# Scores on all eight 64x32 tiles of TensorE, and the feed-forward's sums in the free halves of the attention outputs' banks

## What is computed

```
def attn_layer(x, Wqkv, qs, ksc, Wo):            # 16 heads of 64
    q, k, v = heads(x @ Wqkv)
    q = l2norm(q) * qs;  k = l2norm(k) * ksc
    q, k = rotary(q), rotary(k)
    out = local_attention(q, k, v)               # windows of 32 queries, each sees 64 keys
    return out.reshape(b, n, INNER) @ Wo
def ffn_layer(x, g, bln, W1, b1, W2, b2):
    mu = x.mean(-1, keepdims=True)
    var = ((x - mu) ** 2).mean(-1, keepdims=True)
    xn = (x - mu) / jnp.sqrt(var + 1e-05) * g + bln
    a, gate = jnp.split(xn @ W1 + b1, 2, -1)
    return a * jax.nn.gelu(gate, approximate=False) @ W2 + b2
for i in range(DEPTH):                           # 6 layers, run twice in all
    x = attn_layer(shift_tokens(x), ...) + x
    x = ffn_layer(shift_tokens(x), ...) + x
```

## Time and profile before

| | us |
|---|---|
| median of 3 runs (lowest, highest) | 3282.68 (3281.99, 3286.73) |
| the profiled execution's own time | 3285.78 |
| its span, first to last instruction | 3284.0 |
| PE busy, share of the span | 3149.2 (96%) |
| DVE, POOL, ACT busy | 2675.4 (81%), 2593.5 (79%), 2355.0 (72%) |

### The profile page before, as it was taken

How to read it: one execution, slowest core, us unless ns; L and a number is a source line. 1 busy time by engine, 2 the same in 40 slices (tenths; PEclk the granted TensorE clock), 3 DMA queues, 4 the chain that set the end, 5 groups by cost and what they waited for, 6 DMA issues and landing times.

```text
span 3284.0 us, 149930 instructions
## 1 busy us (share of the span) xinstructions
PE 3149.2 (96%) x63424; PEld 2623.0 (80%) x63424; DVE 2675.4 (81%) x4403; ACT 2355.0 (72%) x4536; POOL 2593.5 (79%) x2894
## 2 busy tenths in 40 slices
PE   5999999999999999999779999999999999999997
PEld 4888888888888888888668888888888888888885
DVE  3888888888888888888558888888888888888884
ACT  3777777777777777777537777777777777777774
POOL 5987887888788878887349888878887888788772
PEclk7999999999999999999879999999999999999998
DMA  2221222222222222221112222222212222221211
GB/s 82 78 59 53 70 60 56 65 66 53 65 68 53 63 67 56 65 67 48 33 27 77 58 56 68 63 53 69 65 50 68 65 54 68 62 59 49 55 50 37
DMA packets 117857, 195.41 MB, mean 60 GB/s; under 512 B 23756, under 2 KB 36552, under 8 KB 117192
## 3 DMA queue, kind: packets, MB, share of 16 engines
q1 hardware_dynamic: 117192, 185.82, 21.2%
HBM read 33.71 MB, written 1.05 MB: 11 GB/s over the span
## 4 chain that ended last, share of the span: by engine, by line
PE 67%; DVE 17%; POOL 7%; issue 5%; ACT 2%; DVEq 0%; POOLq 0%; DMA 0%; ACTq 0%; SPq 0%
PE s_ps L925 8%; PE tr L969 7%; PE o_ps L954 7%; PE tr L938 5%; DVE ss_floor L721 4%; PE f_ps L1015 4%; PE qk_ps L866 4%; PE tr L866 4%; PE qk_ps L867 3%; PE qk_ps L868 3%; PE tr L893 3%; PE tr L906 3%; DVE rotated L714 3%; DVE rotated L708 2%; POOL rotated L420 2%
## 5 line engine op out<-in xcount | busy, mean ns | idle before, releaser
L420 POOL TENSOR_TENSOR rotated<-rotated 128x1024 f32<-128x1024 f32 x384 | 915.3, 2383 | 23.3 <-DVE rotated L714 23.3
L449 POOL TENSOR_TENSOR rotated<-rotated,rn 128x1024 f32<-128x1024 f32 x384 | 730.6, 1903 | 30.1
L426 POOL TENSOR_TENSOR prob<-prob,rden 128x512 f32<-128x512 f32 x384 | 436.5, 1137 | 326.7 <-DVE rden L746 325.7
L528 ACT ACTIVATE sq<-qk_ps 128x1024 f32<-128x1024 f32 x384 | 393.3, 1024 | 281.1 <-PE qk_ps L868 192.9
L708 DVE TENSOR_TENSOR rotated<-qk_ps,rot 128x1024 f32<-128x1024 f32 x384 | 469.3, 1222 | 140.4 <-ACT sq L528 126.4
L714 DVE TENSOR_TENSOR rotated<-qk_ps,rot 128x512 f32<-128x512 f32 x768 | 490.7, 680 | 0.0
L925 PEld LDWEIGHTS s_ps<-kt,qt 64*32 64x32 f32 x24576 | 361.4, 107 | 142.4 <-issue 126.3
L721 DVE TENSOR_REDUCE ss_floor<-sq 128x16 f32<-128x1024 f32 x384 | 464.1, 1209 | 0.4
L574 ACT ACTIVATE pt<-tr 128x512 f32<-128x512 f32 x384 | 229.3, 597 | 321.7 <-PE tr L938 320.3
L925 PE MATMUL s_ps<-kt,qt 64*32 64x64 f32 x24576 | 424.9, 218 | 1.7 <-issue 1.2
L969 PE MATMUL tr<-ot,wo 128*128 128x128 f32 x3072 | 406.7, 275 | 0.0
(11 more groups left out here) (152 smaller groups left out, 6949.9 us busy)
## 6 DMA issues: line engine op xcount, KB each, us to landing
vs<-vn SPq DMA_DIRECT2D x384, 192.0 KB, 2.5
vs<-vtail SPq DMA_DIRECT2D x384, 64.0 KB, 2.0
vtail<-vn SPq DMA_DIRECT2D x384, 64.0 KB, 2.2
staging<-layer_wqkv_dram SPq DMA_DIRECT2D x72, 256.0 KB, 3.0
wo<-layer_wo_dram SPq DMA_DIRECT2D x12, 512.0 KB, 3.9
xs<-xa SPq DMA_DIRECT2D x48, 128.0 KB, 2.3
fs<-xa SPq DMA_DIRECT2D x48, 128.0 KB, 2.3
xs<-xa SPq DMA_DIRECT2D x48, 127.8 KB, 2.4
```

The costliest lines, as they stand in the source:

```text
L420: nc.gpsimd.tensor_tensor(rot_c[h], rot_c[h], rot_s[h], ALU.add).then_inc(rot_added, 1)
L426: nc.gpsimd.tensor_tensor(prob[h][:, :, :], prob[h][:, :, :], rden[h][:, :].unsqueeze(2).to_broadcast([P, 2 * PAIRS, KEYS]), ALU.mult).the ...
L449: nc.gpsimd.tensor_tensor(folded, folded, rn[:, :].unsqueeze(2).to_broadcast([P, 2 * UH, DH]), ALU.mult).then_inc(qkn_ready, 1)
```

## The change

Three things are edited. **Scores:** `s_ps` becomes two banks, one for each row half, 256 columns of each in use; the column group becomes `c = 2 * ws + a0`, with a0 the parity of the pair, so that all eight tiles are used, in an order in which eight products in a row take eight tiles. The mask, maxima, differences and the index of the transposed weights follow that layout. **Banks:** `f_ps` loses its bank; it is now columns 256 to 511 of the two banks of the outputs (`of_ps`; `o_ps` is columns 0 to 255). The feed-forward's products are therefore made in two halves of 256 columns, and the up and gate parts of its gated products lie in different banks. **Waits:** since TensorE may now write outputs into a bank that DVE reads for the feed-forward, `weigh_values` gets waits, in slots 5, 7, 1 and 2, for DVE's read of the variances, of the spread, of the gated products and for the add; and `down` waits for ACT's copy of the outputs.

```diff
-        tr0, tr1, s_ps, f_ps = (... psum_tensor(n, [P, 512], F32) for n in ("tr0", "tr1", "s_ps", "f_ps"))
-        gated_banks = [f_ps, tr0, tr1]
+        s_ps, of_ps, qk_ps = (ctx.enter_context(nc.psum_tensor(n, [P, 2, 512], F32)) for n in ("s_ps", "of_ps", "qk_ps"))
+        score_rows = s_ps[:, :, 0:PAIRS * KEYS].rearrange("p a (r k) -> p a r k", k=KEYS)
+        o_ps = of_ps[:, :, 0:HS]
+        f_ps = of_ps[:, :, HS:SEQ]
+        gated_up = [f_ps[:, 0, :], tr0[:, 0:HS], tr1[:, 0:HS]]
+        gated_gate = [f_ps[:, 1, :], tr0[:, HS:SEQ], tr1[:, HS:SEQ]]
...
-            for a in range(PAIRS):
+            for a1 in range(2):
                 for gg in range(2):
                     for ws in range(2):
-                        for hp in range(2):
-                            w, c = 2 * gg + ws, 2 * ws + hp
+                        for a0 in range(2):
+                            for hp in range(2):
+                                a, w, c = 2 * a1 + a0, 2 * gg + ws, 2 * ws + a0
...
-                                    s_ps[c * WIN:(c + 1) * WIN, (2 * a + gg) * KEYS:(2 * a + gg + 1) * KEYS],
+                                        s_ps[c * WIN:(c + 1) * WIN, hp, (2 * a1 + gg) * KEYS:(2 * a1 + gg + 1) * KEYS],
...
-            def weigh_values(U):
-                TG, h = U // 2, U % 2
+            def weigh_values(p, U):
+                TG, h, n = U // 2, U % 2, U + 2
+                if (it := ffn_of(p, n, VAR_AT + 1)) is not None:
+                    pe.wait_ge(fvar_ready, ONE + it + 1)
+                if (it := ffn_of(p, n, SPREAD_AT + 1)) is not None:
+                    pe.wait_ge(fn_ready, ONE + it + 1)
+                if (it := ffn_of(p, n, GATED_AT + 1)) is not None:
+                    pe.wait_ge(hid_ready, ONE + 2 * NCH * (it + 1))
+                if (it := ffn_of(p, n, ADD_AT)) is not None:
+                    pe.wait_ge(xa_ready, ONE + it + 1)
                 pe.wait_ge(pt_ready, ONE + U + 1)
...
-            def down(it):
+            def down(p, n, it):
+                pe.wait_ge(ot_ready, ONE + min(n - 1, (p + 1) * UPP))
                 pe.wait_ge(w2_in, 16 * NCH * (it // SEQS + 1))
                 pe.wait_ge(hid_ready, ONE + 2 * NCH * (it + 1))
                 for j, (c, m) in enumerate(CHUNKS):
-                    last = nc.tensor.matmul(f_ps[:, :], w2[0:m, j, :], hid[j][0:m, :], start=j == 0, stop=j == NCH - 1)
+                    for i in range(2):
+                        last = nc.tensor.matmul(f_ps[:, i, :], w2[0:m, j, :], hid[j][0:m, i * HS:(i + 1) * HS],
+                                                start=j == 0, stop=j == NCH - 1)
```

More of the change, by code:

```diff
@@ L782, in add_ffn @@
                 dve.wait_ge(fy_ready, ONE + it + 1)
-                nc.vector.scalar_tensor_tensor(xa[:, s, :], f_ps[:, :], vecs[:, l, 2:3], xa[:, s, :], ALU.add, ALU.add).then_inc(xa_ready, 1)
+                halves = xa[:, s, :].rearrange("p (a n) -> p a n", a=2)
+                nc.vector.scalar_tensor_tensor(halves, f_ps, vecs[:, l, 2:3], halves, ALU.add, ALU.add).then_inc(xa_ready, 1)
             for p in range(PASSES):
@@ L917, in scores @@
                 pe.wait_ge(kt_ready, ONE + U + 1)
[L918 removed]
+                for a1 in range(2):
                     for gg in range(2):
                         for ws in range(2):
[L921 to L928 removed]
+                            for a0 in range(2):
+                                for hp in range(2):
+                                    a, w, c = 2 * a1 + a0, 2 * gg + ws, 2 * ws + a0
+                                    rows = slice(hp * DH, (hp + 1) * DH)
+                                    at = t * P + w * WIN
+                                    last = nc.tensor.matmul(
+                                        s_ps[c * WIN:(c + 1) * WIN, hp, (2 * a1 + gg) * KEYS:(2 * a1 + gg + 1) * KEYS],
+                                        qt[h][rows, a, w * WIN:(w + 1) * WIN], kt[h][rows, a, at:at + KEYS],
+                                        start=False, stop=True, skip_group_check=True)
                 last.then_inc(s_ready, 1)
@@ L955, in weigh_values @@
                                     o_ps[hp * DH:(hp + 1) * DH, gg, at:at + WIN], (vn if ws else vs)[h][rows, 2 * a + hp, :],
-                                    pt[h][rows, a, c * WIN:(c + 1) * WIN], start=True, stop=True, skip_group_check=True)
+                                    pt[h][rows, 2 * hp + a // 2, c * WIN:(c + 1) * WIN], start=True, stop=True, skip_group_check=True)
                 last.then_inc(o_ready, 1)
@@ L975, in centre @@
                 pe.wait_ge(xa_ready, ONE + it)
-                nc.tensor.matmul(f_ps[:, :], centre_mat[:, :], fs[:, :], start=True, stop=True).then_inc(fcen_ready, 1)
+                for i in range(2):
+                    last = nc.tensor.matmul(f_ps[:, i, :], centre_mat[:, :], fs[:, i * HS:(i + 1) * HS], start=True, stop=True)
+                last.then_inc(fcen_ready, 1)
             def variances(it):
@@ L980, in variances @@
                 for c in range(TPS):
-                    last = nc.tensor.matmul(f_ps[:, c:c + 1], fsq[:, c * P:(c + 1) * P], mean_mat[:, 0:1], start=True, stop=True)
+                    last = nc.tensor.matmul(f_ps[:, 0, c:c + 1], fsq[:, c * P:(c + 1) * P], mean_mat[:, 0:1], start=True, stop=True)
                 last.then_inc(fvarp_ready, 1)
@@ L1003, in gated @@
                     for part in range(2):
-                        dst = gated_banks[i % 3][0:m, part * HS:(part + 1) * HS]
+                        dst = (gated_gate if part else gated_up)[i % 3][0:m, :]
                         cols = slice(part * HID + c, part * HID + c + m)
@@ L1030, in _ @@
                     if live(p, n - 2):
-                        weigh_values(n - 2)
+                        weigh_values(p, n - 2)
                     if live(p, n):
@@ L1035, in _ @@
                     if (it := ffn_of(p, n, DOWN_AT)) is not None:
-                        down(it)
+                        down(p, n, it)
                     if live(p, n - 1):
```

53 lines of the change are left out of this document (24 added, 29 removed).

## The result

| | before | changed |
|---|---|---|
| median, us (lowest, highest; runs) | 3282.34 (3278.64, 3286.73; 4) | 3332.88 (3329.8, 3343.14; 4) |
| ratio to before, 95% interval | | 1.0159 [1.0133, 1.0185] |
| span of the profiled execution, us | 3284.0 | 3329.1 |

What follows compares the result with a forecast made beforehand. TensorE was taken as the bound, DVE and POOL close behind. 11 x (0 + 0.6 + 1.4) - 15 x 0.3 = 17.5, plus 48 x 0.03 for the halves, gave +19 us: 3302 us predicted, range 3265 to 3345.

Steps and rivals of the forecast that it cites:

- The bound: Whole kernel: TensorE sets the pace, busy 96% of the span, with DVE and POOL following at 85% and 83%.
- The wait for the add: Slot 2: the outputs' products wait for DVE's feed-forward add and start 1.58 us later, in all 48 sequences.
- The wait for the outputs: Slot 1: the down product waits for ACT's copy of the outputs and starts 0.62 us later.
- How fast eight tiles are: Scores of each unit: the pace doubles, 0.46 instead of 0.88 us, saving 0.42 us a unit.
- the torn group: An interrupted scores group, six records started within 0.07 us, read as evidence that tiles take work independently.
- the second rival: Scores: eight tiles are no faster, TensorE admits four records at a time, group stays 1.10 us; 3376 us, chance 0.1.
- the walk: Slot-by-slot sum over a sequence: TensorE alone ends at -1.0 us, then what POOL and DVE hold back is added.
- What DVE and POOL let through: Slots where the transposes of the weights wait for POOL, or DVE leads: part of TensorE's saving is held back.
- the four kinds: A layer's first to fourth sequences, forecast to change by 0, +1.4, +0.6 and -0.3 us.
- The signs to look for: Profile after: scores' group about 0.68 us, 48 waits each for add and copy, more POOL waits, PE some 91% busy.
- The clock: TensorE's granted clock, read at 1.00, its upper level of 2.4 GHz, with nothing left to give.
- The bounds: Scores: the saving for each unit lies between nothing and 0.45 us; 0.42 was taken.

Runs made afterwards that it cites:

- x_early: Changed kernel with DVE's feed-forward add moved from slot 2 to slot 1, behind the differences: 3255.44 us, ratio to before 0.992.
- x_lighter: Kernel before and changed kernel, both with POOL's low parts of next layers' weights and rotary tables cut to 16 columns: 3248.42 and 3284.75 us.
- x_split: Changed kernel with the scores in two halves of 32 records, before and behind the last of the v product's three matmuls: 3391.35 us, single run.
- x_four: Changed kernel with the scores' products reordered so that sixteen in a row take only four of the eight tiles: 3366.21 us, ratio to before 1.0264.

## What the prediction had right, and the step that failed

- **The bound**: right. TensorE was the bound, and gains of 0.24 us in plain slots go through to the time.
- **The wait for the add**: right. 1.58 us forecast, 1.57 in the slots; 65.1 us as a wait, 77 in x_early, part of it the clock. It stands 44 times, not in all 48 sequences as forecast.
- **The wait for the outputs**: right. The down product starts 1.64 us after the scores began, for 1.03: 0.61, forecast 0.62.
- **How fast eight tiles are: this step failed.** "I take the pace to double ... 0.46 instead of 0.88 us", a saving of 161 us if all counted. It is 0.64, and 89 us. Tiles do take work independently, and eight records run at once, as the torn group said; the second rival with its limit of four is refuted (a group of 1.10 was its mark, 0.86 came). But I took the pace of eight tiles to be the only limit, where a second one comes in at the 33rd record, by all that the runs show the supply of instructions. Seven units of a sequence bring 0.24 instead of 0.42 (the eighth is waited away either way): 7 x 0.18 = 1.3 us. TensorE's own sum is +1.58 + 0.62 - 0.35 - 7 x 0.24 = +0.17 us a sequence, where the walk ended at -1.0: 8 us in all instead of -48.
- **What DVE and POOL let through**: right in kind, too large in size. From slot 1 to slot 1 of the next sequence, the four kinds changed by +0.57, +1.45, +1.12 and +0.25 us (first to fourth; sums of the table's rows). Forecast were 0, +1.4, +0.6 and -0.3. The part held by POOL and DVE, over +0.17, is 0.4, 1.3, 1.0 and 0.1; in the walk, over -1.0, it was 1.0, 2.4, 1.6 and 0.7. That is some 33 us in all where the walk had 65 (the walk's kinds, 11 of each of the first three and 15 of the fourth). What isn't saved can't be held: the first error of 56 us made the second smaller, and more than half of it was hidden. The second sequence, in which POOL leads throughout, came out right for that reason. With POOL's extra work cut (x_lighter) some 14 of the 33 are left (22 in the slots less TensorE's own 8); by this reckoning they belong to POOL's and DVE's work of every slot.
- **The signs to look for**: PE's share fell to 92% (some 91 forecast), waits for POOL's L426 rose from 13 to 67, and the down product waits 46 times; the group of 0.68 us did not come.
- **The clock** was read as having "nothing left to give". It had something to lose: some 9 us, in no term of the sum.
- **The sum**: 12 x (0.57 + 1.45 + 1.12 + 0.25) = 41 us, and 9 for the clock, less some 5 at the starts and ends of the passes (the first two sequences of a pass have no feed-forward in slots 0 and 1 and so no wait): 45. Forecast 19.
- **The bounds**: the saving was put between 0 and 0.45, and the value taken from its upper end. That the time still lies in the range is partly luck: the pace was too fast by 56 us in TensorE's sum, and what POOL and DVE hold was too large by some 30, and the two errors point opposite ways.

Still open is what limits the group from the 33rd record on. x_split shows that a pause brings the full pace back, and that it is not the place of the data; the loads that break off with the matmuls speak for the supply of instructions. No run varies the number of instructions or how they are fetched, and of the pace of refilling there is only this kernel's, 31 starts in 0.38 us. That the lowered clock comes from the two waits is argued from its place (slot 1 in all seven) and from x_early, where one of them is gone and no such stretch is left; it wasn't tried by itself.

## What to carry to other kernels

A group of small matmuls may get faster by more tiles only for its first records (here 32 of 64): look for the pace of starts in a group that is already fast, and take the doubling of a pace as an upper bound, not as the value. When two uses begin to share a bank, look first whether the reader can be moved into a gap: here two such moves, and that of fn_lo, turned 50 us lost into 75 won against the kernel before. The kernel before gets 42 us by two of the three moves, so ask of every gain whether it needs the change. And where the engine that sets the pace gets faster in every slot, list the slots in which another engine already follows it within that margin; those gave nothing here.

## What the runs showed of the hardware

- Eight products on eight 64x32 tiles run at once: eight records start within 0.05 us, each recorded with 0.22 to 0.24. In x_four records start from 0.27 us on between those of the first four tiles, which go on to 0.44 (64 starts in 0.77 us, not 0.88). By the program's order these are products on idle tiles that pass earlier ones waiting for theirs. Starts strictly in program order, as the Trainium skill has them in TensorE: Matmul & The Clock Gate, Part 3 (The mechanism), would have kept the 0.88; for tiles of one group the measurement decides against it.
- In a group on eight tiles 32 matmuls, with 32 weight loads, start at 7.7 ns a matmul record, and the next ones at 12 ns; after a pause filled by one full-width matmul the pace is 7.7 again (x_split). The Trainium skill, Advanced Engine Details and Errata, Engine Queue Depths, gives TensorE's queue a depth of 64 ("complicated with tiling"). The trace agrees in so far as 32 loads and 32 matmuls are 64; no run here shows the queue itself.
- The granted clock can fall to 1.2 GHz for some 3 to 4 us after two short waits, 0.57 and 1.51 us, in a kernel whose TensorE is busy for 92% of the time, and not at every repetition: 7 of 44.
- A DVE operation (fn_lo) that takes 0.70 us at best takes 1.9 when it starts 1.4 us before the end of POOL's add of the rotated parts: in 44 of 44 cases it ends 0.55 to 0.56 us after that add, whenever it began. Moved behind the rotation, with no other change, it takes 0.74 on average.
